# Attention values on four column tiles, built on chip: one change to a gated cross-attention and routed FFN kernel

## The chip, the cores and the metric

The kernel runs on one core of a Trainium2 chip. The metric is device time in microseconds (us) of one execution, the median of the runs shown. The engines of the core are named as in the profile: PE (TensorE matmuls), PEld (TensorE weight loads), DVE (VectorE), ACT (ScalarE), POOL (GpSimd) and SP (SyncE, which here only issues DMAs).

## The reference

```python
# x: 8 batches x 256 tokens x 256; ctx_768: 8 x 77 keys x 192; 16 heads of 16; FFN hidden 1024; 2 experts
q = (x @ wq + bq).reshape(B, Sq, H, D).transpose(0, 2, 1, 3)
k = (y @ wk + bk).reshape(B, -1, H, D).transpose(0, 2, 1, 3)
v = (y @ wv + bv).reshape(B, -1, H, D).transpose(0, 2, 1, 3)
scores = einsum('bhqd,bhkd->bhqk', q, k) / sqrt(D)
attn = softmax(scores, axis=-1)
out = einsum('bhqk,bhkd->bhqd', attn, v)
out = out.transpose(0, 2, 1, 3).reshape(B, Sq, E) @ wo + bo
# whole model:
x = x + tanh(g_xattn[0]) * xattn(layernorm(x), ctx_768)
x = x + tanh(g_ffn[0]) * ffn(layernorm(x))   # shared FFN + one of two experts per token (top-1 of a gate)
```

All products whose inputs are cut into a high and a low fp32r part take three fp32r matmuls (high by high, low by high, high by low). The scores of batch 0, the key, value and context projections, all transposes and the products with the values take plain fp32.

## The kernel before, in words

Batches are the outer loop of the attention. For each batch the kernel normalises 256 tokens (`nm`), transposes them (`in`), projects queries (`qy`) and then works on four quarters `k` = 0 to 3: two token tiles `t` by two groups `g` of 8 heads. One quarter is a row of 616 = 8 x 77 probabilities per token. Its steps are: scores on PE (`sc`), maxima on DVE (`sm`, L1246), subtraction on DVE (`ss`, L1258) followed by one exponential on ACT (`ex`, L937), or, for the ten quarters in `FOLDED`, eight exponentials of 77 columns on ACT straight out of PSUM (L947), sums and reciprocals on DVE (`su`, L1264 and L1268), and the division on POOL (`di`, L690).

The 616 columns are then cut into five chunks of keys by heads: four of 128 and a middle one of 104. PE transposes each chunk for both token tiles (`tn`, L1668; the probabilities are the stationary operand and the identity matrix is the moving one), two chunks to a PSUM bank, and ACT copies the bank to `pT` (`te`, L956). `attend` (`va`, L1672) multiplies `pT` with a block-diagonal matrix of values `v_diag`: chunks 0 and 1 hold the first four heads of a group, so they need only output columns 0 to 63, and chunks 3 and 4 only columns 64 to 127. The middle chunk holds parts of both and needs all 128 columns. That gives eight matmuls on 64-column tiles of the array and two on all 128 columns, each with 256 moving columns of fp32. ACT and DVE cut the result into high and low parts (`vae`, `val`), and PE projects it (`ou`).

The diagonal layout of the values is made through memory: POOL clears one buffer of `v_diag`, SP writes it to `v_dram` twice (`vz`, L454), writes each batch's values into the diagonal with two DMAs (`vw`, L484), and reads the block back with three (`vr`, L498). The transposed context `yT` lies in the second buffer of `v_diag` until the projections are done. The keys go through `k_dram` too: two DMAs out (`kw`) and eight per batch back in (`kr`, L481).

The order of the work is written out by hand, one list for each engine (L80 to L139). Each engine takes the steps of its list strictly in order. SP's list, around the change, is:

```python
fl.0 kw.0 vz.0 vz.1 kw.1 kr.1 kr.2 wd.0 vw.0 wd.1 vw.1 vr.0 kr.3 vw.2 vr.1 vr.2 kr.4 ...
```

`wd.n` (L516) loads a 1 MB FFN weight. `wd.0` and `wd.1` fill the two halves of `stage` with the shared weights. ACT rounds them in `wh.n` (L1003, its ACTIVATE on L1012), which waits for the load's semaphore. ACT's list around it is:

```python
... te.0.2.0 te.0.3.1 ex.1.2 ine.3.0 wh.1 te.0.4.1 nm.5 ex.1.3 q32.3.0 nm.6 qe.3 ine.4.1 ex.2.0 ex.2.1 vae.0.0 ...
```

and PE's is:

```python
... in.3.0 tn.0.4.1 sc.2.0 qy.3.0 in.4.1 sc.2.1 va.0.0 tn.1.0.1 ...
```

Here `in.4.1` writes the bank that `tn.0.4.1` filled, so it waits until ACT has done `te.0.4.1`. After the attention the shared FFN (`h`, `y`) and then nine rounds of routed FFN follow, up to the end.

Of the kernel before, what the change touches and what calls it, by code (L numbers as in the profile page):

```python
# [5 lines left out]
F32 = mybir.dt.float32  # L6
# [3 lines left out]
ALU = mybir.AluOpType  # L10
# [3 lines left out]
P = 128  # L14
# [24 lines left out]
MIDDLE = CHUNKS // 2  # L39
ROWS = [GK - (CHUNKS - 1) * P if c == MIDDLE else P for c in range(CHUNKS)]  # L40
ROW0 = [sum(ROWS[:c]) for c in range(CHUNKS)]
CK = 96
# [18 lines left out]
SEAM_OPS = 7  # L61

# [74 lines left out]
    fl.0 kw.0 vz.0 vz.1 kw.1 kr.1 kr.2 wd.0 vw.0 wd.1 vw.1 vr.0 kr.3 vw.2 vr.1 vr.2 kr.4 vw.3 wd.3 vw.4 vr.3  # L137
    kr.5 vr.4 wd.2 vw.5 vw.6 vr.5 kr.6 vw.7 ps.0 kr.7 vr.6 vr.7 ps.1 wd.4 wd.5 ps.2 ps.3 xs ps.4
# [24 lines left out]
def build(nc, x, ctx_768, g_xattn, g_ffn, wq, bq, wk, bk, wv, bv, wo, bo,  # L163
          gate_w, w1, b1, w2, b2, sw1, sb1, sw2, sb2, out):
    k_dram = nc.dram_tensor("k_dram", (P, 2 * GROUPS, BATCHES * KEYS), F32).ap()
    v_rows = nc.dram_tensor("v_rows", (2, GK, GROUPS, P), F32)
    v_dram = v_rows.ap()
# [9 lines left out]
    with ctx:  # L177
# [3 lines left out]
        def sb(name, shape, dt=F32, scope=ctx):  # L181
# [99 lines left out]
        yT = v_diag[0:CK + 1, 1, :, :, :].rearrange("p c g f -> p (c g f)")[:, 0:CKC * BATCHES * KEYS].rearrange(  # L281
            "p (k n) -> p k n", k=CKC)
# [46 lines left out]
        v_zeroed = [sem(f"v_zeroed{n}") for n in range(2)]  # L329
        v_out = [sem(f"v_out{n}") for n in range(2)]  # L330
# [108 lines left out]
        def _(sp):  # L439
# [44 lines left out]
            def values_out(b):  # L484

                n = b % 2
                sp.wait_ge(v_32, b // 2 + 1)
                if b < 2:
                    sp.wait_ge(v_zeroed[n], 16 * 2)
                else:  # L490
                    sp.wait_ge(v_in[n], 16 * 3 * (b // 2))
                for g in range(GROUPS):
                    diagonal = bass.AP(v_rows, n * GK * GROUPS * P + g * P,
                                       [[GROUPS * P, KEYS], [KEYS * GROUPS * P + HEAD_DIM, HG], [1, HEAD_DIM]])
                    sp.dma_start(diagonal, v32[:, b // 2, n, g * P:(g + 1) * P].rearrange("k (h f) -> k h f", h=HG)
                                 ).then_inc(v_out[n], 16)

            def values_in(b):  # L498

                n = b % 2  # L500
                sp.wait_ge(v_out[n], 16 * GROUPS * (b // 2 + 1))
                if b == 0:
                    sp.wait_ge(v_zeroed[0], 16 * 2)
                    sp.wait_ge(v_zeroed[1], 16 * 2)
                if b == 1:
                    sp.wait_ge(v_ps, BATCHES // 2)
                if b >= 2:
                    sp.wait_ge(o_ps, b - 1)
                for c in (0, MIDDLE + 1):
                    sp.dma_start(v_diag[:, n, c:c + MIDDLE, :, :].rearrange("p c g f -> p c (g f)"),  # L510
                                 v_dram[n, ROW0[c]:ROW0[c] + MIDDLE * P].rearrange("(c p) g f -> p c (g f)", p=P)
                                 ).then_inc(v_in[n], 16)
                sp.dma_start(v_diag[0:ROWS[MIDDLE], n, MIDDLE, :, :].rearrange("p g f -> p (g f)"),
                             v_dram[n, ROW0[MIDDLE]:ROW0[MIDDLE + 1]].rearrange("p g f -> p (g f)")).then_inc(v_in[n], 16)

# [35 lines left out]
            for step, at in walk(SP_ORDER):  # L551
                if step == "vz":
                    zero_values(*at)
# [4 lines left out]
                if step == "vw":  # L558
                    values_out(*at)
# [48 lines left out]
        def _(pool):  # L608
# [12 lines left out]
            nc.gpsimd.memset(v_diag[:, 0, :, :, :], 0.0).then_inc(cleared[1], 1)  # L621
# [226 lines left out]
        def _(act):  # L848
# [1055 lines left out]
```

## Time and profile before

| | |
|---|---|
| median of 3 runs | 337.58 us (336.97 to 338.42) |
| profiled execution, span from first to last instruction | 339.1 us |
| profiled execution's own time beside its span | not given by the page; the span stands for it, 1.5 us above the median |
| PE busy | 318.2 us (94%) |
| DVE, ACT, POOL busy | 227.9, 215.6, 184.0 us |
| mean granted PE clock | 0.980 |
| DMA | 38150 packets, 35.68 MB; 16608 packets under 512 B |

A busy share is the time in which an engine has an instruction under way, so a busy PE may still have idle columns or tiles. The mean clock of 0.980 comes mainly from one stretch at half rate around 31.8 to 42 us.

### The profile page before, as it was taken

What the parts mean: (1) busy time and instruction counts of PE and PEld (TensorE: products, weight loads), DVE (VectorE), ACT (ScalarE), POOL (GpSimd) and SP (SyncE); (2) the same over time, 40 slices, a digit from 0 to 9 for tenths busy, and PEclk for the clock granted to TensorE, in tenths of its full rate; (3) what the DMA queues carried; (4) which work ended last, traced back from release to release, by engine and by line L of the source; (5) the groups of instructions that cost most, each with busy time, mean ns of one, the idle gap of its engine ahead of it and who ended that gap; (6) DMA issues with size and microseconds to landing.
All of it is one profiled execution on the core that took longest, in us unless ns stands there. A gap on an engine that the chain in (4) does not pass through costs nothing.

```text
span 339.1 us, 7286 instructions
## 1 busy us (share of the span) xinstructions
PE 318.2 (94%) x2363; PEld 282.2 (83%) x2363; DVE 227.9 (67%) x516; ACT 215.6 (64%) x483; POOL 184.0 (54%) x261
## 2 busy tenths in 40 slices
PE   6997879899999999999999999999999999999993
PEld 5764666678988877788799889999999999999992
DVE  6999689999878899796767675534333544353463
ACT  2855898976786665658957584547546546464652
POOL 8226979885652564757371177432255536534542
PEclk9998599999999999999999999999999999999997
DMA  7992855274422030053160100315246233212300
GB/s 191 299 340 38 241 126 160 42 198 128 109 80 56 2 97 29 0 139 121 15 240 2 62 2 31 127 32 188 79 168 217 66 151 93 77 35 75 92 32 28
DMA packets 38150, 35.68 MB, mean 105 GB/s; under 512 B 16608, under 2 KB 35060, under 8 KB 37613
## 3 DMA queue, kind: packets, MB, share of 16 engines
q1 hardware_dynamic: 34568, 27.36, 28.5%
q0 software_dynamic: 2720, 7.32, 6.4%
q10 hardware_dynamic: 837, 0.67, 0.8%
q8 instruction: 14, 0.23, 0.3%
q14 instruction: 11, 0.09, 0.1%
HBM read 21.20 MB, written 9.85 MB: 92 GB/s over the span
## 4 chain that ended last, share of the span: by engine, by line
PE 61%; DVE 15%; ACT 8%; issue 7%; DMA 5%; POOL 1%; POOLq 1%; SPq 1%; DVEq 0%; ACTq 0%
PE y_ps L1535 20%; PE h_ps L1535 17%; PE bank L1535 9%; PE s_ps L1535 9%; DMA x_all<-in_x 5%; PE bank L1668 4%; ACT probs L947 2%; DVE rsum L1264 2%; DVE smax L1246 1%; DVE probs L1258 1%; DVE stats L1147 1%; DVE other_sum L1232 1%; ACT pT L956 1%; DVE hT_lo L1469 1%; ACT xn L898 1%
## 5 line engine op out<-in xcount | busy, mean ns | idle before, releaser
L690 POOL TENSOR_TENSOR probs<-probs,rinv 128x616 f32<-128x616 f32 x32 | 39.1, 1223 | 37.8 <-DVE rinv L1268 37.5
L1535 PE MATMUL y_ps<-sw,hT_hi 128*128 128x256 f32 x272 | 57.1, 290 | 1.2 <-DVE hT_lo L1513 1.2
L1535 PE MATMUL y_ps<-ew,hT_hi 128*128 128x256 f32 x256 | 54.1, 286 | 1.8 <-DVE hT_lo L1469 1.7
L1469 DVE TENSOR_TENSOR hT_lo<-h,hT_hi 128x256 fp32r<-128x256 f32 x64 | 29.2, 457 | 38.5 <-ACT h L1086 35.2
L1535 PEld LDWEIGHTS y_ps<-sw,hT_hi 128*128 128x128 f32 x272 | 44.9, 191 | 2.9 <-DVE hT_lo L1513 1.8
L1535 PEld LDWEIGHTS y_ps<-ew,hT_hi 128*128 128x128 f32 x256 | 42.4, 188 | 3.0 <-DVE hT_lo L1469 3.0
L1535 PE MATMUL h_ps<-x2T_hi,sw 128*128 128x512 f32 (+1 forms) x160 | 43.6, 359 | 0.1
L1083 ACT ACTIVATE hT_hi<-h_ps,vec_cols 128x256 fp32r<-128x256 f32 x32 | 15.2, 475 | 39.5 <-PE h_ps L1535 35.3
L995 ACT ACTIVATE hT_hi<-h_ps,vec_cols 128x512 fp32r<-128x512 f32 (+1 forms) x40 | 24.6, 614 | 21.9 <-PE h_ps L1535 17.3
L1535 PE MATMUL y_ps<-sw,hT_lo 128*128 128x256 f32 x136 | 38.4, 282 | 0.0
L1535 PE MATMUL y_ps<-ew,hT_lo 128*128 128x256 f32 x128 | 35.9, 280 | 0.0
L1264 DVE TENSOR_REDUCE rsum<-probs 128x8 f32<-128x616 f32 x32 | 25.1, 785 | 9.3 <-ACT probs L947 5.9
L821 POOL DMA_INDIRECT out<-final,scatter_token x16 | 18.0, 1127 | 24.6 <-DVE final L1488 19.2
L1535 PEld LDWEIGHTS h_ps<-x2T_hi,sw 128*128 128x128 f32 x160 | 26.8, 190 | 3.5 <-issue 0.8
L716 POOL TENSOR_TENSOR hT_lo<-h,hT_hi 128x512 fp32r<-128x512 f32 (+1 forms) x15 | 17.2, 1151 | 21.9 <-ACT h L1000 21.7
L1535 PE MATMUL h_ps<-x2T_lo,sw 128*128 128x512 f32 (+1 forms) x80 | 27.8, 348 | 0.0
L956 ACT ACTIVATE pT<-bank 128x512 f32<-128x512 f32 x40 | 23.7, 611 | 5.9 <-PE bank L1668 5.4
L1535 PE MATMUL h_ps<-xsT_parts,ew 128*128 x192 | 26.5, 280 | 0.0
L1535 PE MATMUL s_ps<-xsT_parts,ew 128*128 x192 | 26.4, 279 | 0.0
L1379 DVE TENSOR_TENSOR hT_lo<-h,hT_hi 128x512 fp32r<-128x512 f32 (+1 forms) x25 | 16.2, 654 | 15.0 <-ACT h L1000 15.0
L1535 PEld LDWEIGHTS y_ps<-sw,hT_lo 128*128 128x128 f32 x136 | 26.0, 191 | 0.2
L1668 PE MATMUL bank<-ident,probs 128*128 128x128 f32 (+1 forms) x160 | 24.3, 284 | 1.4 <-ACT pT L956 1.0
(206 smaller groups left out, 837.1 us busy)
## 6 DMA issues: line engine op xcount, KB each, us to landing
v_diag<-v_rows SPq DMA_DIRECT2D x16, 256.0 KB
stage<-in_L_ffn_w SPq DMA_DIRECT2D x4, 1024.0 KB, 5.6
sw<-ew SPq DMA_DIRECT2D x4, 1024.0 KB
xs<-sorted_dram SPq DMA_DIRECT2D x8, 257.0 KB
stage<-in_L_ffn_sw SPq DMA_DIRECT2D x2, 1024.0 KB, 6.6
x_all<-in_x SPq DMA_DIRECT2D x1, 1536.0 KB, 9.8
part_dram<-x_all SPq DMA_DIRECT2D x3, 512.0 KB, 2.9
k_dram<-probs SPq DMA_DIRECT2D x2, 616.0 KB, 5.9
```

The lines of the kernel that those rows point to most:

```text
L690: nc.gpsimd.tensor_tensor(pq, pq, rinv[:, b % 2, k, :].unsqueeze(2).to_broadcast([P, HG, KEYS]), ALU.mult).then_inc(p_ready, 1)
L716: nc.gpsimd.tensor_tensor(hT[1][:, q % HB, 0:width], h32[:, q % 2, 0:width], hT[0][:, q % HB, 0:width], ALU.subtract).then_inc(h_lo_pool, 1)
L821: pool.indirect_dma_start(out=out[:, :], out_offset=bass.IndirectOffsetOnAxis(ap=scatter_token[:, t:t + 1], axis=0), in_=final[:, t, :], i ...
L947: ins = nc.scalar.activation(to[:, h * KEYS:(h + 1) * KEYS], score_banks(quarter)[:, h // HH, keys], ACT.Exp, bias=smax[:, b % 2, k, h:h + 1])
L956: nc.scalar.activation(pT[:, 2 * u:2 * u + 2, :].rearrange("p c s -> p (c s)"), bank[m][:, :], ACT.Copy).then_inc(pT_sb, 1)
L995: nc.scalar.activation(hT[0][:, q % HB, 0:width], h_ps[:, q % 2, 0:width], ACT.Relu, bias=b1_sb[:, 0, c:c + 1]).then_inc(h_hi, 1)
L1083: nc.scalar.activation(hT[0][:, c % HB, 0:RTOK], hidden_bank(c % 4)[:, 0:RTOK], ACT.Relu, bias=b1_sb[:, 1 + e, c:c + 1]).then_inc(h_hi, 1)
L1264: nc.vector.tensor_reduce(out=rsum[:, b % 2, k, :], in_=probs[:, b % 2, k, :].rearrange("p (h k) -> p h k", k=KEYS), axis=AX_X, op=ALU.add ...
L1379: nc.vector.tensor_tensor(hT[1][:, q % HB, 0:width], h32[:, q % 2, 0:width], hT[0][:, q % HB, 0:width], ALU.subtract).then_inc(h_lo, 1)
L1469: nc.vector.tensor_tensor(hT[1][:, c % HB, 0:RTOK], h32[:, c % 2, 0:RTOK], hT[0][:, c % HB, 0:RTOK], ALU.subtract).then_inc(h_lo, 1)
L1535: return nc.tensor.matmul(out_, lhsT, rhs, start=start, stop=stop, **kw)
L1668: ins = nc.tensor.transpose(bank[m][0:ROWS[c], v * SEQ + t * P:v * SEQ + (t + 1) * P], probs[:, b % 2, g * TB + t, ROW0[c]:ROW0[c] + ROWS[ ...
```

## The change

Heads are taken in pairs. One group of 8 heads has four pairs, and a pair has 154 = 128 + 26 key columns. The keys of two pairs are interleaved in `probs`: the column of (pair, head in pair, key) is `n * 308 + q * 154 + k * 2 + i`, with `n` the half of the group, `i` the pair in that half and `q` the head in the pair. Subtraction, exponentials, sums and division address `probs` through this layout. The first (or last) 128 keys of each pair are now every second column, and the middle 104 columns are what is left of all four pairs. The transposes read their four chunks of 128 with a step of two elements.

`attend` then has, per group, four matmuls on four 32-column tiles of the array (one per pair, with 128 rows) and one on all 128 columns with 104 rows. That is again eight and two matmuls a batch.

The values are no longer written to memory. POOL clears `v_pair` and `v_left` once, and SP copies each batch's values from `v32` in SBUF to their places with eight DMAs (four for `v_pair`, four for `v_left`), in runs of 16 elements. `vz` and `vw` are gone, `yT` has a buffer of its own, and SP's list has `vr.0 vr.1` between `wd.0` and `wd.1`. The lists of the other engines are unchanged.

```diff
 SP_ORDER = """
-    fl.0 kw.0 vz.0 vz.1 kw.1 kr.1 kr.2 wd.0 vw.0 wd.1 vw.1 vr.0 kr.3 vw.2 vr.1 vr.2 kr.4 vw.3 wd.3 vw.4 vr.3
-    kr.5 vr.4 wd.2 vw.5 vw.6 vr.5 kr.6 vw.7 ps.0 kr.7 vr.6 vr.7 ps.1 wd.4 wd.5 ps.2 ps.3 xs ps.4
+    fl.0 kw.0 kw.1 kr.1 kr.2 wd.0 vr.0 vr.1 wd.1 kr.3 vr.2 kr.4 wd.3 vr.3 kr.5 vr.4 wd.2 vr.5 kr.6 ps.0 kr.7
+    vr.6 vr.7 ps.1 wd.4 wd.5 ps.2 ps.3 xs ps.4
 """
...
+        def heads_of(b, k):
+            return probs[:, b % 2, k, :].rearrange("p (n q k i) -> p n i q k", n=2, q=2, i=HP)
+        def by_head(rows):
+            return rows.rearrange("p (n i q) -> p n i q", n=2, q=2)
...
             def values_in(b):
                 n = b % 2
-                sp.wait_ge(v_out[n], 16 * GROUPS * (b // 2 + 1))
...
-                for c in (0, MIDDLE + 1):
-                    sp.dma_start(v_diag[:, n, c:c + MIDDLE, :, :] ..., v_dram[n, ...]).then_inc(v_in[n], 16)
-                sp.dma_start(v_diag[0:ROWS[MIDDLE], n, MIDDLE, :, :] ..., v_dram[n, ...]).then_inc(v_in[n], 16)
+                sp.wait_ge(cleared[1], 2)
+                sp.wait_ge(v_32, b // 2 + 1)
+                if b >= 2:
+                    sp.wait_ge(o_ps, b - 1)
+                split = P - KEYS
+                for half, parity, to, key in ((0, 0, 0, 0), (0, 1, KEYS, 0), (1, 0, 0, LEFT), (1, 1, split, 0)):
+                    rows = KEYS if half == parity else split
+                    heads = v32[key:key + rows, b // 2, n, half, :].rearrange("k (c q f) -> k c q f", q=2, f=HEAD_DIM)
+                    cols = slice(parity * HEAD_DIM, (parity + 1) * HEAD_DIM)
+                    sp.dma_start(v_pair[to:to + rows, n, half, :, cols], heads[:, :, parity, :]).then_inc(v_in[n], 16)
+                for half in range(2):
+                    key = split if half == 0 else 0
+                    left = v32[key:key + LEFT, b // 2, n, half, :].rearrange("k (g d) -> k g d", g=GROUPS)
+                    for i in range(HP):
+                        first = (2 * i + 1 - half) * HEAD_DIM
+                        rows = slice(half * HP * LEFT + i, (half + 1) * HP * LEFT, HP)
+                        sp.dma_start(v_left[rows, n, :, half * HR + first:half * HR + first + HEAD_DIM],
+                                     left[:, :, first:first + HEAD_DIM]).then_inc(v_in[n], 16)
...
             def turn(b, u, m):
+                        if c < PAIRS:
+                            first = c // HP * (GK // 2 + HP * LEFT) + c % HP
+                            cols = slice(first, first + HP * (P - 1) + 1, HP)
+                        else:
+                            cols = slice(HP * P, HP * P + ROWS[c])
...
             def attend(b, m):
                 for g in range(GROUPS):
-                    for n in range(MIDDLE):
-                        for half in range(2):
-                            c, cols = half * (MIDDLE + 1) + n, slice(half * HR, (half + 1) * HR)
-                            mm(bank[m][cols, g * SEQ:(g + 1) * SEQ], v_diag[:, b % 2, c, g, cols],
-                               pT[:, g * CHUNKS + c, :], g == 0 and n == 0, False, skip_group_check=True)
+                    for i in range(PAIRS):
+                        cols = slice(i * PD, (i + 1) * PD)
+                        mm(bank[m][cols, g * SEQ:(g + 1) * SEQ], v_pair[:, b % 2, i // HP, g * HP + i % HP, :],
+                           pT[:, g * CHUNKS + i, :], g == 0, False, skip_group_check=True)
```

## Rows read from the trace of the kernel before

**Rows 1.** The page: busy time of each engine; granted PE clock in 40 slices.
```profile
PE 318.2 (94%) x2363; PEld 282.2 (83%) x2363; DVE 227.9 (67%) x516; ACT 215.6 (64%) x483; POOL 184.0 (54%) x261
...
PEclk9998599999999999999999999999999999999997
```
**Rows 2.** The chain of waits: shares, then pieces (start us, us, what).
```profile
PE 61%; DVE 15%; ACT 8%; issue 7%; DMA 5%; POOL 1%; POOLq 1%; SPq 1%; DVEq 0%; ACTq 0%
...
74.73 2.94 PE bank L1535 x20
...
80.70 0.44 PE bank L1668 x4
...
84.50 0.72 PE y_ps L1535 x6
...
186.38 2.94 PE bank L1535 x20
```
**Rows 3.** Busy time by stretch; then PEclk, DMA share, GB/s.
```profile
26.60:31.80 5.20, 3.35 (x12) 1.81 (x10) 4.91 (x12) 2.60 (x9) 3.69 (x14) 1.00 0.20 32
31.80:42.00 10.20, 7.96 (x38) 6.82 (x40) 7.60 (x13) 8.30 (x23) 9.37 (x12) 0.50 0.73 193
...
45.60:78.00 32.40, 28.80 (x222) 21.64 (x219) 29.46 (x49) 27.58 (x59) 28.60 (x40) 1.00 0.48 118
78.00:113.00 35.00, 35.00 (x273) 30.69 (x273) 29.92 (x62) 26.65 (x64) 16.53 (x27) 1.00 0.36 89
113.00:151.00 38.00, 36.69 (x269) 30.18 (x269) 33.21 (x83) 21.73 (x44) 23.24 (x32) 1.00 0.23 59
151.00:228.00 77.00, 77.00 (x548) 69.41 (x547) 49.59 (x114) 50.67 (x100) 39.04 (x56) 1.00 0.21 69
```
**Rows 4.** Timeline of PE (start us, us): value projection, last attend, what follows it.
```profile
16.91 1.90 PE L1535 MATMUL y_ps<-stage,v_diag 97*77 97x256 f32 x8
...
186.31 3.01 PE L1535 MATMUL bank<-pT,v_diag 128*64 128x256 f32 x20
188.97 0.82 PE L1535 MATMUL h_ps<-x2T_hi,sw 128*128 128x512 f32 x2
```
**Rows 5.** Groups by form: busy us, mean ns of one, idle before.
```profile
L690 POOL TENSOR_TENSOR probs<-probs,rinv 128x616 f32<-128x616 f32 x32 | 39.1, 1223 | 37.8 <-DVE rinv L1268 37.5
L1264 DVE TENSOR_REDUCE rsum<-probs 128x8 f32<-128x616 f32 x32 | 25.1, 785 | 9.3 <-ACT probs L947 5.9 <-ACT probs L937 3.3
...
L1668 PEld LDWEIGHTS bank<-ident,probs 128*128 128x128 f32 x128 | 15.4, 144 | 3.5 <-issue 1.2 <-ACT pT L956 0.8 <-DVE x2T_lo L1293 0.5
...
L1535 PEld LDWEIGHTS y_ps<-sw,hT_hi 128*128 128x128 f32 x256 | 41.9, 191 | 0.9 <-issue 0.5
```
**Rows 6.** Timeline of SP's DMA issues (start us, us), 22 to 41 us.
```profile
22.61 11.74 SPq L481 DMA_DIRECT2D k_own<-k_dram  x16
34.45 0.53 SPq L530 DMA_DIRECT2D stage<-in_L_ffn_sw  x1
35.08 0.89 SPq L495 DMA_DIRECT2D v_rows<-v  x2
36.02 2.38 SPq L530 DMA_DIRECT2D stage<-in_L_ffn_sw  x1
38.50 2.24 SPq L495 DMA_DIRECT2D v_rows<-v  x2
```
**Rows 7.** Weight loads into `stage`: issue to landing.
```profile
DMA to landing us min/median/max: 4.9/5.7/8.0
```
**Rows 8.** Timeline of ACT around `wh.1` (start us, us).
```profile
45.12 0.60 ACT L907 ACTIVATE xnT_hi<-bank 128x512 fp32r<-128x512 f32 x1
45.60 1.92 ACT L1012 ACTIVATE sw<-stage 128x2048 fp32r<-128x2048 f32 x1
47.40 0.61 ACT L956 ACTIVATE pT<-bank 128x512 f32<-128x512 f32 x1
```
**Rows 9.** Timeline of PE: `in.4.1`, which needs the copy after `wh.1`.
```profile
48.10 0.62 PE L1607 MATMUL bank<-ident,xn 128*128 128x128 f32 x4
```

More of the change, by code:

```diff
@@ L37 @@
 TURNS = GROUPS * CHUNKS // 2
-MIDDLE = CHUNKS // 2
-ROWS = [GK - (CHUNKS - 1) * P if c == MIDDLE else P for c in range(CHUNKS)]
-ROW0 = [sum(ROWS[:c]) for c in range(CHUNKS)]
+PAIRS = HG // 2
+HP = PAIRS // 2
+PK = 2 * KEYS
+LEFT = PK - P
+ROWS = [P] * PAIRS + [PAIRS * LEFT]
+PD = 2 * HEAD_DIM
 CK = 96
@@ L61 @@
 SEAM_OPS = 7
+VALUE_LOADS = 4 + PAIRS
 UNITS = [[0], [1, 2], [3, 4], [5, 6], [7]]
@@ L328, in build @@
         v_32 = sem("v_32")
-        v_zeroed = [sem(f"v_zeroed{n}") for n in range(2)]
-        v_out = [sem(f"v_out{n}") for n in range(2)]
         v_in = [sem(f"v_in{n}") for n in range(2)]
@@ L482, in keys_in @@
                                  ).then_inc(k_in[n], 16)
[L484 to L496, printed above, removed]
@@ L557, in _ @@
                     keys_in(*at)
-                if step == "vw":
-                    values_out(*at)
                 if step == "vr":
@@ L688, in divide @@
                 pool.wait_ge(p_rinv, 4 * b + k + 1)
-                pq = probs[:, b % 2, k, :].rearrange("p (h k) -> p h k", k=KEYS)
-                nc.gpsimd.tensor_tensor(pq, pq, rinv[:, b % 2, k, :].unsqueeze(2).to_broadcast([P, HG, KEYS]),
-                                        ALU.mult).then_inc(p_ready, 1)
+                pq = heads_of(b, k)
+                inverse = by_head(rinv[:, b % 2, k, :]).unsqueeze(4).to_broadcast([P, 2, HP, 2, KEYS])
+                nc.gpsimd.tensor_tensor(pq, pq, inverse, ALU.mult).then_inc(p_ready, 1)
             def scatter(u):
@@ L887, in value_rows @@
                 act.wait_ge(v_ps, j + 1)
-                nc.scalar.activation(v32[:, j, :, :].rearrange("k n d -> k (n d)"), value_bank(j), ACT.Copy
+                nc.scalar.activation(v32[:, j, :, :, :].rearrange("k n m d -> k (n m d)"), value_bank(j), ACT.Copy
                                      ).then_inc(v_32, 1)
@@ L946, in exponents @@
                     keys = slice(h % HH * KEYS, (h % HH + 1) * KEYS)
-                    ins = nc.scalar.activation(to[:, h * KEYS:(h + 1) * KEYS], score_banks(quarter)[:, h // HH, keys],
+                    ins = nc.scalar.activation(heads_of(b, k)[:, h // HH, h % HH // 2, h % 2, :],
+                                               score_banks(quarter)[:, h // HH, keys],
                                                ACT.Exp, bias=smax[:, b % 2, k, h:h + 1])
@@ L1008, in weights_hi @@
                     for half in range(2):
-                        act.wait_ge(v_out[half], 16 * GROUPS * BATCHES // 2)
+                        act.wait_ge(v_in[half], 16 * VALUE_LOADS * BATCHES // 2)
                 if n >= 4:
@@ L1256, in shifted @@
                 dve.wait_ge(s_max, 4 * b + k + 1)
-                m = smax[:, b % 2, k, :].rearrange("p (n h) -> p n h", n=2).unsqueeze(3).to_broadcast([P, 2, HH, KEYS])
-                nc.vector.tensor_tensor(probs[:, b % 2, k, :].rearrange("p (n h k) -> p n h k", n=2, k=KEYS),
-                                        score_heads(4 * b + k), m, ALU.subtract).then_inc(s_shifted, 1)
+                m = by_head(smax[:, b % 2, k, :]).unsqueeze(4).to_broadcast([P, 2, HP, 2, KEYS])
+                nc.vector.tensor_tensor(heads_of(b, k), score_heads(4 * b + k).rearrange("p n (i q) k -> p n i q k", q=2),
+                                        m, ALU.subtract).then_inc(s_shifted, 1)
             def sums(b, k):
                 dve.wait_ge(p_exp, 4 * b + k + 1)
-                nc.vector.tensor_reduce(out=rsum[:, b % 2, k, :],
-                                        in_=probs[:, b % 2, k, :].rearrange("p (h k) -> p h k", k=KEYS),
-                                        axis=AX_X, op=ALU.add).then_inc(p_sum, 1)
+                nc.vector.tensor_reduce(out=by_head(rsum[:, b % 2, k, :]), in_=heads_of(b, k), axis=AX_X, op=ALU.add
+                                        ).then_inc(p_sum, 1)
                 dve.wait_ge(p_sum, 4 * b + k + 1)
@@ L1596, in values_in @@
                         ins = mm(value_bank(j)[:, n * DIM:(n + 1) * DIM], yT[rows, k, b * KEYS:(b + 1) * KEYS],
-                                 wv_sb[rows, k, :], k == 0, k == CKC - 1)
+                                 wv_sb[rows, k, :].rearrange("p (g m d) -> p m g d", g=GROUPS, m=2), k == 0,
+                                 k == CKC - 1)
                 ins.then_inc(v_ps, 1)
```

40 lines of the change are left out of this document (10 added, 30 removed).

## The prediction, made before the changed kernel was run

> **What bounds the kernel now.** I read the page first, then the chain of waits, then the busy time by stretch, and last the timelines of PE, SP and ACT around the edited steps. PE is busy for 94% of the span and the others for 54 to 67% [rows 1], and 61% of the chain is PE [rows 2]. By stretch it differs [rows 3]. From 45.6 to 78 us nobody leads: PE is busy 28.8 of 32.4 us, DVE 29.5, ACT 27.6, POOL 28.6, so a delay of any of them is handed on. From 78 to 113 and from 151 to 228 us PE is never idle. From 113 to 151 PE has 1.3 us idle in 38, DVE is busy 33.2, and the chain there runs mostly over DVE. After 228 us comes the routed FFN, which the change doesn't touch.
>
> **PE's part of the change.** Each attend has 20 matmul records (two to an fp32 matmul). The last one begins at 186.31 and the next step at 188.97, so it takes 2.66 us [rows 4]. One fp32 record of 256 columns alone in the array costs 0.217 us: eight records of the value projection take 1.90, the last being 0.38 long, and (1.90 - 0.38) / 7 = 0.217 [rows 4]. Twenty in a row would take 4.34 us. At 2.66 the sixteen 64-column records must run in pairs: 8 slots + 4 full ones = 12 slots x 0.217 = 2.60. On four 32-column tiles the sixteen records fit 4 slots, plus 4 full ones: 8 x 0.217 + 0.06 = 1.80. Each attend saves 0.86 us at full clock. The trace shows no four tiles at once, so the bounds are 0 (only two run together) and 0.86; I take 0.86, because two tiles overlap without loss.
>
> The eight attends save 6.9 us of PE time, but not all of it reaches the end. Four of them lie whole on the chain (74.7, 95, 165 and 186 us, of which the first and last stand in [rows 2]): 4 x 0.86 = 3.4 us. The other four lie in the stretches where other engines share the bound [rows 3]; there PE would mostly wait longer. I count a quarter of their 3.4: 0.9. Sum -4.3 us, with bounds 0 and -6.9.
>
> The Trainium skill, TensorE: Matmul & The Clock Gate, "Part 3: Packing small matmuls", gives 2.38 times for three column tiles, not 3. At that efficiency (estimated 79% for four) the sixteen records would take 1.08 instead of 0.86 us and an attend would save 0.65; the sum of the four on the chain would be -2.6 instead of -3.4. The trace's pairs lose nothing, so I stay with the rows.
>
> **The step of two elements.** The stationary loads of 128 of the 160 transposes now read every second element. Now such a load takes 144 ns [rows 5] and transposes follow each other every 0.11 us (0.44 for 4), while a load of 191 ns [rows 5] goes with a spacing of 0.12 us (0.72 for 6) [rows 2]. If the step made the load as slow as that, each transpose would cost 0.01 more: 1.3 us in all, at most. Below nothing there is no reason. The other readers and writers of `probs` are 32 sums of 785 ns, 32 divisions of 1223 ns [rows 5], the subtractions and exponentials. No row has a stepped access, so their bounds are nothing and a doubling of the sums, 25 us of DVE. I take nothing, since number of elements and engine stay the same. The Trainium skill, SBUF — State Buffer, "SBUF: two separate sides", says that two hits per 16-byte line keep full rate; a step of 8 bytes gives exactly two. By that rule the cost is nothing too, but one element further it would not be.
>
> **SP's part, where the change can lose.** Removed: four clearing writes, sixteen diagonal writes, 24 reads of `v_dram`. Added: 64 small copies, eight per batch. Their bytes are nothing (DMA share is 0.2 to 0.5 after 78 us [rows 3]), but SP's issue time and order count. Now SP issues the 16 key DMAs from 22.61 to 34.35, `wd.0` at 34.45, two `vw` at 35.08 and `wd.1` at 36.02 [rows 6]. Afterwards:
>
> - The key DMAs start when `kw.0` has landed instead of behind `vz`, about 1.2 us earlier (21.4), and at their undisturbed pace of 0.635 instead of 11.74 / 16 = 0.73 end at 31.6. So `wd.0` goes out at 31.6, 2.9 us earlier.
> - Then 16 value copies stand before `wd.1`, instead of two. Their price is between 0.45 each (0.89 for two `vw`) and 1.12 (2.24 for two `vw` behind the weights) [rows 6]. Both ends of a copy have three dimensions, as a key DMA has, so I take 0.635: 10.2 us, and `wd.1` goes out at about 42.4 (39.3 to 50).
> - A weight load lands 4.9 to 8.0 us after its issue [rows 7]. With nearly nothing beside it I take 5.4: landing at 47.8.
>
> `wh.1` on ACT needs that load. It runs at 45.60, directly behind other work, so it waits for nothing now [rows 8]. At 47.8 ACT stands for 2.2 us. Behind it on ACT are `te.0.4.1` (47.40), then `nm.5`, `ex.1.3` and the queries; PE's `in.4.1` (48.10 [rows 9]) needs that copy's bank, and the attend of batch 0 comes after it. From there the engines run in lockstep [rows 3]; I let 85% through: +1.9 us. Bounds: 0 (issue at 0.45) and about +8 (every copy at twice its pace).
>
> `kr.3` behind `wd.1` goes out at about 43 against 44 to 45 now. The later copies (`vr.2` on) wait for an attend two batches before their use and have some 10 us or more; 5 us of issue each fit. POOL's clearing has 1024 elements instead of 1280. Nothing else moves. `vr.0` and `vr.1` land before 50 us, where the first attend needs them.
>
> **Sum.** -4.3 + 1.9 = -2.4 us. The profiled span is 339.1, 1.5 above the median of 337.58; the same difference on the median gives **335.2 us**.
>
> **Rivals.**
> - *The weight load comes on time.* The copies cost SP about 0.45 each and `wd.1` lands before 45.6. For it: `vw` went at that pace. Against: their neighbours with two strided sides don't. Only the gain is left: 337.6 - 4.3 = 333.3, to 330.7 if all eight attends count.
> - *The stall grows and takes the clock along (slower).* Copies blocked behind `wd.0`, as `wd.1` and the second `vw` are now (2.38 and 2.24 us [rows 6]), put `wd.1` at 44.5 and its landing at 50: ACT stands 4.4 us, +3.7. PE is then idle from 48.3 for over 4 us. Now, PE was idle 1.85 of 5.2 us before 31.8, and the granted clock was 0.50 (the 1.2 GHz level) for the next 10.2 us [rows 3]. The same again costs half of some 8.5 us of PE work less what was slack, about +3. Result 337.6 - 4.3 + 3.7 + 3 = 340.0. It decides from a `wd.1` issue later than about 43.5 us. Against: the 3.6 us of idle spread over 45.6 to 78 us left the clock at 1.00 [rows 3].
> - *Four tiles run no better than two.* No gain, stall stays: 339.5. For it: no row has four. Against: pairs lose nothing.
> - *The stepped access costs.* A tenth more on sums and divisions and 0.01 on each transpose: 32 x 0.08 + 32 x 0.12, half of it hidden by idle time before them, + 1.3 gives +4: 339.2. Against: none but the absence of any row for it.
>
> **How the numbers follow.** Chances: forecast 0.36, load on time 0.24, stall with clock 0.20, tiles don't overlap 0.08, stepped access 0.12. The range goes from 331.5 (nearly all attends count, no stall) to 341 (stall, clock, and some of the last two). About 0.5% (1.7 us) is what a measurement of this kernel tells from no change, so faster means under 335.9 and slower over 339.3. Faster: 0.27 of the forecast's 0.36, and the 0.24 of the load on time, 0.51. Slower: 0.15 of the clock case, 0.06 and 0.08 of the last two, 0.29. Same: the rest, 0.20.
>
> **What would show it.** In the profile after: each attend 1.80 us from its first record to the next step; transpose loads still near 144 ns and spaced 0.11; `rsum` near 785 and the division near 1223 ns; SP's issue of `wd.1` at about 42.4 and 0.635 per copy; ACT idle about 2.2 us before L1012 at 46 us, with a DMA as releaser; PE's clock 1.00 after 42 us; PE never idle from 78 to 113 us, moved as a whole. The prediction is wrong if the clock falls a second time, if the attends keep 2.66 us, or if 113 to 151 us takes the gain back over DVE.

## The result, and the profile after

The changed kernel took 348.64 us (median of 4 runs, 348.31 to 349.12), the kernel before 338.0 beside it (336.97 to 340.12). The ratio is 1.0318, with a 95% interval of 1.0272 to 1.0363: slower by some 10.6 us, where 335.2 with a range of 331.5 to 341.0 was forecast. The profiled execution of the changed kernel took 349.12 us, 1.8 more than its span of 347.3. (In nearly all other runs on record, too, the time lies 1.7 to 1.9 us above the span. So the execution in the profile of before took about 340.9, and is one of that kernel's slower ones.)

The page after, its first two parts, cut to the rows that answer to [rows 1]:

```profile
PE 317.8 (91%) x2363; PEld 282.0 (81%) x2363; DVE 230.0 (66%) x516; ACT 215.8 (62%) x483; POOL 183.0 (53%) x262
...
PE   7998572989899999899999999999999999999993
...
PEclk9999896999999999999999999999999999999998
DMA  6951422014130102003225010130553362213201
```

PE is busy for as long as before (317.8 against 318.2 us) in a span that is 8.2 us longer, so the loss is idle time. It lies mostly in the seventh slice (52 to 61 us), where PE's digit is 2 and the clock's 6. The chain of waits there has what the chain of before did not have, SP's copies and a weight load (start, duration in us, engine, target):

```profile
48.02 0.83 SPq L501
48.90 7.19 DMA stage<-in_L_ffn_sw
56.31 1.62 issue
```

SP's DMA issues of the changed kernel (start us, us), which answer to [rows 6], and ACT around `wh.1` (now L998), which answers to [rows 8]:

```profile
33.40 0.52 SPq L518 DMA_DIRECT2D stage<-in_L_ffn_sw  x1
34.02 4.36 SPq L494 DMA_DIRECT2D v_pair<-v  x4
38.43 3.47 SPq L501 DMA_DIRECT2D v_left<-v  x4
42.01 3.33 SPq L494 DMA_DIRECT2D v_pair<-v  x4
45.37 3.48 SPq L501 DMA_DIRECT2D v_left<-v  x4
48.90 0.52 SPq L518 DMA_DIRECT2D stage<-in_L_ffn_sw  x1
```

```profile
47.86 0.60 ACT L892 ACTIVATE xnT_hi<-bank 128x512 fp32r<-128x512 f32 x1
56.12 1.91 ACT L998 ACTIVATE sw<-stage 128x2048 fp32r<-128x2048 f32 x1 [7.65 <-DMA stage<-in_L_ffn_sw]
57.93 0.58 ACT L942 ACTIVATE pT<-bank 128x512 f32<-128x512 f32 x1
```

Sixteen value copies took SP from 34.02 to 48.90, 0.93 us each. `wd.1` was issued at 48.90 instead of 36.02, and ACT stood for 7.65 us for it, with everything behind it in ACT's order. PE's timeline shows the same hole, and the busy time by stretch shows what the clock did (columns: stretch, length, busy PE, PEld, DVE, ACT, POOL, PEclk, DMA share, GB/s):

```profile
58.57 1.11 PE L1593 MATMUL bank<-ident,xn 128*128 128x128 f32 x4 [7.56 <-ACT pT L942]
```

```profile
41.60:45.00 3.40, 3.40 (x18) 3.18 (x20) 2.00 (x4) 2.98 (x9) 3.40 (x5) 0.50 0.12 12
...
48.40:55.20 6.80, 2.04 (x18) 1.61 (x14) 3.10 (x6) 0.06 (x1) 3.93 (x5) 1.00 0.59 173
55.20:62.10 6.90, 3.41 (x22) 2.07 (x26) 1.83 (x4) 5.98 (x10) 0.86 (x1) 0.51 0.04 8
```

PE was busy 2.04 of 6.8 us, and then the granted clock fell to the 1.2 GHz level until 62.1. The first such stretch, 10.2 us long in [rows 3], was 3.4 us here, and a second profile of the kernel before (e5 below) has none at all. Where and how long the clock falls early in the kernel differs from one execution to the next.

The attends' own matmuls are as short as forecast, at full clock and with four tiles at once. The groups by form, which answer to [rows 5] (busy us, mean ns of one, idle before):

```profile
L676 POOL TENSOR_TENSOR probs<-probs,rinv 128x616 f32<-128x616 f32 x32 | 39.5, 1237 | 46.7 <-DVE rinv L1253 46.3
L1250 DVE TENSOR_REDUCE rsum<-probs 128x8 f32<-128x616 f32 x32 | 25.2, 786 | 17.2 <-ACT probs L922 11.2 <-ACT probs L932 5.9
...
L1659 PEld LDWEIGHTS bank<-ident,probs 128*128 128x128 f32 x128 | 18.2, 206 | 6.1 <-ACT pT L942 3.1 <-DVE x2T_lo L1278 1.1 <-issue 0.9
...
L1520 PE MATMUL bank<-pT,v_pair 128*32 128x256 f32 x128 | 9.1, 406 | 0.1
```

```profile
73.25 1.07 PE L1520 MATMUL bank<-pT,v_pair 128*32 128x256 f32 x16
74.25 1.13 PE L1520 MATMUL bank<-pT,v_left 104*128 104x256 f32 x4
```

The four full-width records begin 1.00 us after the first of the sixteen, and a chain piece of an attend fell from 2.94 [rows 2] to 2.06 us. Sum and division kept their durations. The stepped loads went from 144 to 206 ns.

Where the difference arises, by landmarks of the profiles (us from the span's start, all read from timelines):

| | before | before, again | after | after, again | e1, `wd.1` first |
|---|---|---|---|---|---|
| first scores of batch 1 | 32.39 | 31.89 | 35.74 | 33.38 | 33.04 |
| `wh.1` on ACT | 45.60 | 43.74 | 56.12 | 54.96 | 45.59 |
| attend of batch 0 | 50.37 | 48.49 | 60.87 | 59.72 | 50.36 |
| fourth store of a part | 228.35 | 226.13 | 238.83 | 237.71 | 228.27 |
| from the attend to that store | 177.98 | 177.64 | 177.96 | 177.99 | 177.91 |
| end | 339.1 | 334.7 | 347.3 | 345.2 | 336.9 |

Everything is lost before the attend of batch 0: 10.5 us in the first pair of profiles, 11.2 in the second. What `wh.1` is late (10.52 us in the first pair) arrives whole at the attend (10.50) and at the last store (10.48). From there to the last store, where 6.9 us of attends were to be saved, the two kernels need the same time within 0.4 us. The routed stage behind it has nothing of the change. It took 107.2 to 110.8 us in the profiles of both kernels, and explains nothing.

### The profile page after: what moved, and what is told of

It is laid out like the page before. It is cut to its first block, busy times and chain, and to the rows that moved or that the text cites. A ratio compares the mean times of both kernels' runs of the same rounds, so it can differ in the third digit from the quotient of the medians.

```text
span 347.3 us, 7297 instructions
## 1 busy us (share of the span) xinstructions
PE 317.8 (91%) x2363; PEld 282.0 (81%) x2363; DVE 230.0 (66%) x516; ACT 215.8 (62%) x483; POOL 183.0 (53%) x262
## 4 chain that ended last, share of the span: by engine, by line
PE 54%; DVE 15%; ACT 8%; issue 8%; SPq 7%; DMA 5%; POOL 1%; POOLq 1%; DVEq 0%; ACTq 0%
PE y_ps L1520 21%; PE h_ps L1520 16%; PE s_ps L1520 7%; PE bank L1520 5%; SPq L479 3%; PE bank L1659 3%; DVE rsum L1250 2%; SPq L494 2%; DMA stage<-in_L_ffn_sw 2%; SPq L501 2%; ACT probs L932 2%; DVE smax L1232 2%; DMA stage<-in_ctx 2%; DVE other_sum L1218 1%; DVE probs L1244 1%
## 5 line engine op out<-in xcount | busy, mean ns | idle before, releaser
L676 POOL TENSOR_TENSOR probs<-probs,rinv 128x616 f32<-128x616 f32 x32 | 39.5, 1237 | 46.7 <-DVE rinv L1253 46.3
L1520 PE MATMUL y_ps<-ew,hT_hi 128*128 128x256 f32 x256 | 53.1, 285 | 0.8 <-DVE hT_lo L1454 0.8
L1454 DVE TENSOR_TENSOR hT_lo<-h,hT_hi 128x256 fp32r<-128x256 f32 x64 | 29.5, 461 | 32.3 <-ACT h L1072 32.0
L1250 DVE TENSOR_REDUCE rsum<-probs 128x8 f32<-128x616 f32 x32 | 25.2, 786 | 17.2 <-ACT probs L922 11.2
L1659 PE MATMUL bank<-ident,probs 128*128 128x128 f32 (+1 forms) x160 | 25.6, 291 | 2.4 <-ACT pT L942 1.6
L1659 PEld LDWEIGHTS bank<-ident,probs 128*128 128x128 f32 (+1 forms) x160 | 21.0, 191 | 6.8 <-ACT pT L942 3.1
```

Source lines behind the costliest of these rows:

```text
L676: nc.gpsimd.tensor_tensor(pq, pq, inverse, ALU.mult).then_inc(p_ready, 1)
L1250: nc.vector.tensor_reduce(out=by_head(rsum[:, b % 2, k, :]), in_=heads_of(b, k), axis=AX_X, op=ALU.add).then_inc(p_sum, 1)
L1454: nc.vector.tensor_tensor(hT[1][:, c % HB, 0:RTOK], h32[:, c % 2, 0:RTOK], hT[0][:, c % HB, 0:RTOK], ALU.subtract).then_inc(h_lo, 1)
L1520: return nc.tensor.matmul(out_, lhsT, rhs, start=start, stop=stop, **kw)
L1659: ins = nc.tensor.transpose(bank[m][0:ROWS[c], v * SEQ + t * P:v * SEQ + (t + 1) * P], probs[:, b % 2, g * TB + t, cols], ident[:, :])
```

## The experiments

Fourteen runs were made. The kernel before ran beside each of them, with medians from 336.75 to 339.45 us by group of runs (e1 to e4, e5 to e8, e9 to e12, e13 and e14), so across groups only ratios are compared. Line numbers are those of the kernel in question.

**e1 and e11: `wd.1` back in its place.**

```diff
-    fl.0 kw.0 kw.1 kr.1 kr.2 wd.0 vr.0 vr.1 wd.1 kr.3
+    fl.0 kw.0 kw.1 kr.1 kr.2 wd.0 wd.1 vr.0 vr.1 kr.3
```

> The changed kernel with one word moved in SP's order: wd.1 goes out directly behind wd.0, ahead of the 16 value copies of vr.0 and vr.1. My theory: the loss is the late weight load (ACT idle 7.65 us before sw<-stage) and the second stretch at half clock that the idle PE brings (55.3 to 62.1 us, worth 3.4). Without it wd.1 is issued near 36, ACT does not wait for it, PE's clock stays at full speed after its first dip, and the time falls from 348.6 by 9 to 11 us to 338 to 340. If the slower start (everything 3 us later at 16 us) is an accident of single executions, 335.5 to 338. Rival: the stall only moves, because the copies now hold back kr.3 and the first attend waits for its values; then no more than half of it goes, 343 or more.

338.69 us, ratio 1.0041 (1.0012 to 1.0071) instead of 1.0318. One word in SP's list gives back 2.8% of the time, some 9.4 us. ACT's timeline of this kernel has no wait before `wh.1`:

```profile
45.59 1.92 ACT L998 ACTIVATE sw<-stage 128x2048 fp32r<-128x2048 f32 x1
```

The copies, now behind the weight load, hold nothing up, so the rival falls. On another chip, with a second profile:

> The kernel with wd.1 first once more, beside the two others on one chip, as their measure and for a second profile of its start. By all theories the ratio of before, 1.004 with 0.003 to either side, and SP past the second load of x at 9.2 to 11.

Ratio 1.0048 (1.0025 to 1.0071), as expected. The 0.4 to 0.5% that stay are real, and with the shorter attends they had to be explained: the sum of the forecast would have this kernel at 333.3.

**e2: half of the copies ahead.** `wd.0 vr.0 wd.1 vr.1`.

> The changed kernel with 8 value copies (vr.0) ahead of wd.1 and 8 (vr.1) behind it. At the 0.93 to 0.98 us per copy that the first eight took, wd.1 is issued at about 41.9 and lands at 47.5 to 49; ACT comes to it at about 48.4. My theory (a threshold: only a load later than ACT's turn costs) says that this is within 1 us of the kernel with wd.1 first. Rival (every copy ahead of the weights costs, since they share SP and the DMA rings): halfway between the two, 343 to 344.

340.14 us, ratio 1.0093 (1.0057 to 1.0128), 1.45 over e1, so it was not quite free and a little outside the 1 us of the theory; the rival's 343 is far off. `wd.1` went out at 41.40 and `wh.1` ran at 46.99, 1.34 us late:

```profile
46.99 1.91 ACT L998 ACTIVATE sw<-stage 128x2048 fp32r<-128x2048 f32 x1 [1.34 <-DMA stage<-in_L_ffn_sw]
```

That the loss is about the stall is chance, though. In this execution the clock fell from 51.4 to 58 us, over the attend of batch 0 and what follows it:

```profile
51.40:58.00 6.60, 6.25 (x32) 3.88 (x33) 5.57 (x11) 5.51 (x10) 5.89 (x7) 0.50 0.17 27
```

From that attend to the next it took 13.57 us instead of the 12.34 of e1, and the fourth store of a part stood at 230.92, 2.65 later than in e1: 1.39 from the stall and 1.23 from the clock. The routed stage, which has nothing of the edit, happened to be 1.35 shorter (107.3 against 108.6). The threshold picture holds, and the point is an issue at about 40 us, since from issue to ACT's copy it took 5.6 us here and ACT's turn comes at 45.6.

**e3: the same delay in the kernel before.** Nothing but `wd.1` is later.

```diff
-    wd.0 vw.0 wd.1 vw.1 vr.0 kr.3
+    wd.0 vw.0 vw.1 vr.0 kr.3 wd.1
```

> The kernel before, with wd.1 moved behind vw.1, vr.0 and kr.3: nothing else is later, only this weight load, issued at about 48 instead of 36 as in the changed kernel. My theory: ACT idles 7 to 9 us before sw<-stage, PE's clock falls to half a second time, and the time rises by 9 to 11 us to 347 to 349. Rival (the changed kernel's loss comes from its copies, stepped accesses or start, and the weight load has slack behind it): at most 3 us, 341 or less.

347.08 us, ratio 1.0297 (1.024 to 1.0354): the late weight load alone makes 9.8 us, where the whole change makes 10.6. Its ACT and PE show the stall and the attend of batch 0 at half clock:

```profile
53.73 1.91 ACT L1012 ACTIVATE sw<-stage 128x2048 fp32r<-128x2048 f32 x1 [8.85 <-DMA stage<-in_L_ffn_sw]
```

```profile
58.48 4.77 PE L1535 MATMUL bank<-pT,v_diag 128*64 128x256 f32 x20
```

The records of this attend span 4.77 us against 3.01 at full clock, and the stretch from it to the next attend was 13.87 us, not 12.35. In the changed kernel the clock falls too, but that stretch is 12.38 us, as with e1 (12.34), and from `wh.1` to the attend it is 4.75 us in it and 4.77 in e1. So the fall of the clock behind the stall cost 1.5 us in e3 and nothing in the changed kernel. What differs in these four profiles, beside the longer attend of e3, is how far the fall reaches beyond the start of the attend: 1.2 us in the profile of after and 1.7 in its repeat, where it cost nothing, and 3.7 in e3 and 6.3 in e2, where it cost 1.5 and 1.2.

**e7: every attend as long as before.** The 16 records on column tiles are issued twice, the second time over the first.

```diff
-                for g in range(GROUPS):
+                for g in [*range(GROUPS)] * 2:
                     for i in range(PAIRS):
```

> The kernel with wd.1 first, with the 16 records on four column tiles of every attend issued twice, the second time over the first: an attend then takes about 2.66 us as in the kernel before, +0.86 each, 6.9 us of PE in all. Theory: nearly all of the attends' gain was hidden, because DVE (its 3.35 us sw<-stage,sw, and the softmax work from 113 to 151 us) ends just behind PE; the time rises by only 0 to 2 us over 338.7, so up to 340.7. Rival (my prediction's step: four attends whole on the chain and a quarter of the rest): +4.3, 343. If all eight are on the path: +6.9, 345.6.

338.5 us, ratio 1.0009 (0.9973 to 1.0045), where e1 and e11 had 1.0041 and 1.0048. So 6.9 us more of PE's work cost nothing that can be measured, the low end of the theory's 0 to 2. The forecast's 4.3 us would have needed a ratio near 1.017 and are excluded. The third attend shows how. In e1, then in e7, PE (and DVE in e1) around it:

```profile
74.72 1.07 PE L1520 MATMUL bank<-pT,v_pair 128*32 128x256 f32 x16
75.72 1.13 PE L1520 MATMUL bank<-pT,v_left 104*128 104x256 f32 x4
77.77 0.47 PE L1520 MATMUL h_ps<-x2T_hi,sw 128*128 128x256 f32 x2 [0.92 <-DVE sw L1382]
...
73.72 3.35 DVE L1382 TENSOR_TENSOR sw<-stage,sw 128x2048 fp32r<-128x2048 f32 x1
76.99 0.68 DVE L1278 TENSOR_TENSOR x2T_lo<-bank,x2T_hi 128x512 fp32r<-128x512 f32 x1
```

```profile
75.10 1.93 PE L1520 MATMUL bank<-pT,v_pair 128*32 128x256 f32 x32
...
76.97 1.13 PE L1520 MATMUL bank<-pT,v_left 104*128 104x256 f32 x4
78.19 0.48 PE L1520 MATMUL h_ps<-x2T_hi,sw 128*128 128x256 f32 x2
```

From the attend's first record to the next step it is 3.05 us with short attends, 3.09 with doubled ones and 3.12 in the kernel before. In the kernel before PE seemed to set the pace without a gap, but DVE's `x2T_lo`, behind the subtraction, ended at 77.68, 0.1 us before PE's next step at 77.78. In e1 it ended at 77.67, again 0.1 us before that step. The last attend is alike. In e1 the next step comes 2.22 us after its first record, not 1.80, 0.1 us behind the end of an `x2T_lo` at 188.96. With doubled attends it comes after 2.65.

**e4: what the step of two costs.**

```diff
-                            cols = slice(first, first + HP * (P - 1) + 1, HP)
+                            cols = slice(c * P, (c + 1) * P)
```

> The kernel with wd.1 first whose 128 transposes of whole chunks read contiguous columns instead of every second one; the pairs of heads are then mixed up, so what is left out is the right order of the keys. Prices the step of two: the loads fall from 206 to about 144 ns. My theory: this costs the chain at most 0.01 to 0.02 us a transpose, 1.3 to 2.5 us in all, so 0 to 2 us faster than the kernel with wd.1 first. Rival (the slower load sets PE's pace wherever transposes stand alone): 62 ns on each of 128, 5 to 8 us faster.

337.1 us, ratio 1.0007 (0.9967 to 1.0048), 1.6 us under e1. The load's row:

```profile
L1659 PEld LDWEIGHTS bank<-ident,probs 128*128 128x128 f32 x128 | 14.3, 140 | 7.4 <-ACT pT L942 3.4 <-DVE xnT_lo L1225 1.3 <-DVE x2T_lo L1278 1.1
```

So the step makes a load 66 ns slower (206 against 140). PE's eight transposes in a row took 0.96 us to the next step in e1 and 0.85 here, 0.014 each, or 1.8 us over all 128 if none is hidden. In the trace, though, 1.17 of the gain lie in one stretch, between the third and the fourth attend (20.24 against 19.07 us), and most of it is no transpose: the sixteen stepped ones of a stretch make 0.22 at 0.014 each. In e1 POOL ran a division beside DVE's subtraction (73.72, 3.35 us, above). That division, then the same two in e4:

```profile
73.68 1.23 POOL L676 TENSOR_TENSOR probs<-probs,rinv 128x616 f32<-128x616 f32 x1
```

```profile
73.42 2.30 DVE L1382 TENSOR_TENSOR sw<-stage,sw 128x2048 fp32r<-128x2048 f32 x1
...
73.51 3.29 POOL L676 TENSOR_TENSOR probs<-probs,rinv 128x616 f32<-128x616 f32 x1
```

One of the two ran at its usual duration, and the other took 1.0 or 2.1 us longer. In e1 POOL was 0.04 us ahead, in e4 DVE 0.09. The pair meets like this in 15 of the 16 profiles (all but e8). DVE took 3.34 to 3.40 us wherever POOL began earlier or at most 0.01 later, and POOL took 3.29 to 3.33 wherever DVE was 0.03 or more ahead. The unchanged kernel before shows both orders: 20.23 us for the stretch in its first profile, where DVE waited, and 19.85 in its second, where POOL did. So the order alone is worth 0.4. And e4, with POOL waiting and short attends, has 19.07 where the kernel before with POOL waiting has 19.85: there the shorter attend shows almost whole (0.78 of 0.86), while with DVE waiting it shows nothing (20.24 against 20.23). That is read from traces; no run fixes the order.

**e8: DVE's subtraction of the weights ahead.**

```diff
-    sm.3.2 ss.3.2 wl.0 n2l.0.0.0
+    wl.0 sm.3.2 ss.3.2 n2l.0.0.0
```

> The kernel with wd.1 first, and DVE's wl.0 (sw<-stage,sw, 3.35 us at 73.7) put ahead of sm.3.2 and ss.3.2, 1.6 us of softmax work. PE waits 0.92 us for it behind the third attend. Theory: PE's wait there goes, and the gain of that attend shows: 0.5 to 0.9 us less, 337.8 to 338.2, more if DVE also starts ahead of POOL's division (with contiguous transposes it started 0.09 us ahead of it and took 2.30 instead of 3.35 us). Rival: the later softmax holds back the next attend, and the time stays at 338.7 or rises by up to 1.6.

340.35 us, ratio 1.0062 (1.0023 to 1.01), so no gain over e1 (1.0041) and perhaps a loss. The subtraction took 2.39 us now, but the stretch from the second to the third attend went from 12.02 to 14.24 us, because PE waits for the softmax that was put behind it:

```profile
76.81 0.41 PE L1520 MATMUL s_ps<-k_own,q_hi 64*128 64x308 f32 x2 [2.05 <-DVE probs L1244]
```

The granted clock then fell to 0.50 (77.4 to 80.7 us), and the first sixteen records of the third attend took 1.87 us instead of 1.00. The rival was right. On DVE, with 29.5 of 32.4 us busy [rows 3], the 3.35 us can't be moved for nothing.

**e5 and e6: both kernels once more, for the start.**

> The kernel before, unchanged, profiled once more, to see what one execution differs from the next. In the profiled execution of before the routed stage (from the last store of a part, 228.35, to the end) took 110.75 us, against 107.2 to 108.6 in four others. If that is chance of single executions it takes 107 to 109 here, and the first attend may begin 1 to 3 us earlier or later than 50.4, with the phase of the clock. If it belongs to the kernel before, 110 to 111 again.

Its time was 336.5 us; the routed stage took 108.6, so the 110.75 was chance.

> The changed kernel, unchanged, profiled once more, for its start: in its profiled execution PE ran its first 14 us at half rate (h_ps<-yT,stage 2.26 us for 4, against 1.20 to 1.28 in the four others) and everything stood 3 us later at 16 us. If that is chance, h_ps takes about 1.2 here and the first keys are stored near 16 us. If it belongs to the change, 2.26 and 18.8 again. The ACT idle before sw<-stage: near 7.7 in either case, or up to 10 when the start is early, since SP's queue is bound by its own issues after 34 us.

Its time was 346.99 us. PE's slow start (matmuls at twice their duration, while the profile gives a granted clock of 1.00) was chance as well. The first keys went out at 16.45. The ACT wait was 9.63 us, near the upper figure: the earlier ACT comes to `wh.1`, the longer it waits, because SP has its own pace.

A smaller delay of the start stayed. In all seven profiles of changed kernels so far (after, its repeat, e1, e2, e4, e7, e8) SP passed its wait on the second load of `x` at 9.15 to 10.99 us. In three of the kernel before or its variant (before, e5, e3) it was 8.14 to 9.26. POOL clears 1024 columns where it cleared 1280, so its loads of bias and gate rows start at 5.60 instead of 5.77. Four more kernels vary when these loads start.

**e9, e10, e12, e14: POOL's loads later; e13: earlier.** The edit of e9 and e14, in the kernel of e1 (e10 has it four times; e12 has two clearings of `v_diag` more in the kernel before):

```diff
+            for n in range(1):
+                nc.gpsimd.memset(v_left[:, :, :, :], 0.0).then_inc(held, 1)
+                pool.wait_ge(held, n + 1)
```

> The kernel with wd.1 first, with one more clearing of v_left (0.46 us of POOL) ahead of POOL's loads. What is open: with wd.1 first the time is still 1.4 us over before. In three profiles of before SP passed its wait on the second load of x at 8.1 to 9.3 us, in seven of the changed kernel at 9.2 to 11.0, and the first scores come 1 us later. POOL clears 1024 columns instead of 1280 and so starts its row loads at 5.60 instead of 5.77. Theory: those 768 KB get ahead of parts of the x load; with the extra clearing they start 0.3 us later than in before, SP passes at 8.1 to 9.3 and the time falls by about 1.3 us to that of before (ratio 1.000). Rival: the order of 0.17 us has nothing to do with it; SP passes at 9.2 to 11 and the ratio stays 1.004.

> The same with four more clearings (about 2.2 us of POOL). Theory: as with one, and perhaps a little more, since the x load then has the DMA engines to itself: ratio 0.996 to 1.000. Against it: the row loads and the gains then land late, and ACT waits for the gains. Rival: ratio 1.004 or more.

> The kernel before with its clearing of v_diag done three times (2.2 us more of POOL) ahead of POOL's loads, to see whether their start matters to that kernel too. Theory: its x load is already ahead, so nothing to 0.5 us is gained (ratio 0.998 to 1.001). Rival: the row loads are needed late only and any delay of them helps, ratio 0.996 or less; or the later gains cost, 1.002 or more.

> The kernel before, in which POOL clears only 1024 of the 1280 columns of v_diag ahead of its row loads, as the changed kernel clears 1024, and the rest behind them. Theory (the row loads get ahead of the second load of x): POOL's row loads start near 5.55 instead of 5.77, SP passes its wait on that load at 9.2 to 11 instead of 8.1 to 9.3, the first scores come at 32.7 to 33.7 instead of 31.9 to 32.8, and the time rises by about 1 us (ratio 1.002 to 1.004). Rival (what delays the start is something else in the changed kernel, where its tiles lie for one): start and ratio as before, 1.000.

> The kernel with wd.1 first and one more clearing ahead of POOL's loads, again, beside e13. Theory: SP passes at 8.1 to 9.3 and the first scores at 31.9 to 32.5, as in its first profile (8.73 and 32.18); the ratio 1.000 to 1.003, against 1.0041 and 1.0048 without the clearing. Rival: 1.004 or more, and the early start of the first profile was chance.

| | row loads start | SP past the second x load | first scores | ratio |
|---|---|---|---|---|
| e13, before, clears 1024 first | 5.55 | 9.99 | 33.42 | 1.0031 (1.0004 to 1.0058) |
| e1 | 5.60 | 9.65 | 33.04 | 1.0041 (1.0012 to 1.0071) |
| e11 | 5.60 | 9.70 | 32.86 | 1.0048 (1.0025 to 1.0071) |
| before, again | 5.78 | 8.27 | 31.89 | 1 |
| e9 | 6.19 | 8.73 | 32.18 | 1.0028 (1.0001 to 1.0056) |
| e14 | 6.18 | 9.13 | 32.45 | 1.0019 (0.9995 to 1.0044) |
| e10 | 7.97 | 8.25 | 32.69 | 1.0043 (1.0012 to 1.0074) |
| e12, before | 8.25 | 9.04 | 32.80 | 1.0001 (0.9973 to 1.003) |

The rows behind the first and the fifth line, SP, POOL and ACT of e13, then of e9:

```profile
9.99 0.39 SPq L452 DMA_DIRECT2D x_all<-in_x  x1
...
5.55 0.57 POOL L643 DMA_DIRECT2D gate_rows<-in_L_ffn_gate_w  x1
...
9.32 0.63 ACT L872 ACTIVATE wqo_hi<-stage 128x512 fp32r<-128x512 f32 x1 [1.54 <-DMA stage<-in_L_xattn_wq]
```

```profile
8.73 0.38 SPq L460 DMA_DIRECT2D x_all<-in_x  x1
...
6.19 0.57 POOL L632 DMA_DIRECT2D gate_rows<-in_L_ffn_gate_w  x1
...
7.95 0.62 ACT L859 ACTIVATE wqo_hi<-stage 128x512 fp32r<-128x512 f32 x1
```

In nine profiles with the row loads before 5.65 us the wait ended at 9.15 to 10.99, in seven with them at 5.77 or later at 8.14 to 9.26. SP's wait is only a mark of the traffic. What an engine waits for in eight of the nine is the query weight `wq`, a load of 256 KB that SP issues at 2.5 us: ACT's `wqo_hi` waits 0.34 to 1.76 us for it, and not in any of the seven. (In the ninth, e4, the second x load itself is the latest of all, 10.99.) Put into the kernel before, the earlier loads made it slower (e13, 1.0031, an interval just clear of 1; its theory held). Both runs of the kernel with half a microsecond of delay (e9 and e14) lie under e1 and e11, but the intervals overlap; e14 is as its theory had it, and the 1.000 expected of e9 did not come. A delay of 2 us gives nothing more (e10, where the theory's 0.996 to 1.000 failed and its rival of 1.004 was right; e12, as expected): the first scores then come at 32.7 to 32.8 although the x load is early. So the direction rests on the profiles and on e13. The size, 1 us in the profiles, is within the intervals of the times.

No version beat the kernel before. Of the changed ones with the right order of the keys e7, with its doubled attends, has the lowest ratio (1.0009), then e14 (1.0019), and the times tell neither from it. A layout that shortens the attends without the step of two was not run.

## Why the prediction was wrong

- **What bounds the kernel: wrong.** "From 78 to 113 and from 151 to 228 us PE is never idle" was read as PE being the bound. e7 refutes it for the whole: with 0.86 us more of PE's work in each of the eight attends the time is the same. A shorter attend turned into waits: behind DVE's `sw` (0.92 us, third attend) and for DVE's `x2T_lo` (0.65 us after the sixth, against 0.23 in the kernel before). In e1 only the last two attends gave something, about half of their 0.86 each.
- **The attend's own cost: right.** 1.80 forecast, 0.86 saved; measured 2.06 against 2.94 in the chain, 0.88. The rival of two tiles falls. By the estimate from the 2.38 times of the Trainium skill, TensorE: Matmul & The Clock Gate, "Part 3: Packing small matmuls", the sixteen records would have taken 1.08 us (0.868 / 0.79 is 1.10); they took 1.00 to the next record, between that and the 0.87 of full overlap. The second sixteen of e7 add 0.87 (1.87 for 32), so all but 0.13 us overlaps fully.
- **Its effect: the step that failed first.** "Four of them lie whole on the chain", −4.3 us in all. Measured: nothing that can be told from zero. By stretches from one attend to the next, e1 against e7: −0.42 and −0.54 behind the last two attends, +0.55 between the fifth and the sixth, about nothing elsewhere. The +0.55 comes on DVE. In before and e7 three `other_sum` operations took 1.52 us and the four behind them 2.48. In e1 the three took 2.54 and the four 2.03, with POOL's `q_lo` at 125.19 in between. That is read from traces; no run moved POOL there.
- **SP's copies: the mis-sized term, and most of the miss.** `wh.1` was forecast 2.2 us late (47.8 instead of 45.6) and started at 56.12, 10.5 late. Of the 8.3 us between, 4.7 are the copies: 0.635 us each was taken from the key DMAs, with bounds of 0.45 and 1.12, and it was 0.93 (`v_left` 0.87, `v_pair` 0.83 to 1.09). Another 1.8 is the start of the copies (34.02 instead of 32.2) and 1.8 the landing (7.19 us instead of 5.4 for this load; in the repeat it took 5.6). The issue at 48.9 instead of 42.4 lay inside the bounds of 39.3 to 50, but past the point where ACT waits each further microsecond counts in full.
- **"I let 85% through": wrong, all of it went through.** 10.52 us at `wh.1`, 10.50 at the attend, 10.48 at the last store; in e2, 1.40 and 1.39 at the first two.
- **The rival "The stall grows and takes the clock along"** named the mechanism, and its point of decision (an issue later than 43.5) was passed by 5 us. It priced it at 340.0, since it stopped at an issue at 44.5 and took a gain of 4.3 off. Its clock term of +3 was nothing in the changed kernel. With the measured 10.5 us of delay, without the gain and without the clock it gives 348.1, and 348.64 was measured.
- **The stepped access: sums and divisions right, the transposing loads wrong.** I let them grow from 144 to 191 at most; they took 206. Per transpose it was 0.014 against the 0.01 allowed. (The rival's sum was off by itself: 3.2 + 1.3 is 4.5, not 4.) The rule cited from the Trainium skill, SBUF — State Buffer, "SBUF: two separate sides" (two hits per 16-byte line keep full rate), held for the engines (rsum 786 against 785 ns), and this load did not keep its duration.
- **POOL's clearing: the step costed at nothing.** "POOL's clearing has 1024 elements instead of 1280. Nothing else moves." What stood behind it on POOL, 768 KB of loads, moved up by 0.17 us and into the way of the `wq` load and the second x load, for about 1 us. With that and key DMAs of 0.67 us each instead of 0.635, `wd.0` came at 33.40, not at 31.6, and still at 33.23 in e1, where PE did not start slowly.

## What to carry to other kernels

Before an engine that is always busy is called the bound, ask of each stretch what its neighbours would show if it were 1 us faster: a neighbour in lockstep with it takes the gain (DVE was busy 87 to 91% of 45.6 to 78 and 113 to 151 us here). Doubling the work in question is a cheap test of that, and can be run before a change is made. Small DMAs on an in-order queue are paid by the issue (0.83 to 1.09 us each for these copies): put them behind every load that an engine waits for, and count what each edit does to the loads at the start.

## What was not expected of the hardware

- Four fp32 matmuls of 256 columns on four 32-column tiles overlap nearly fully: sixteen records in 1.00 us and 32 in 1.87 (e7), against 3.47 for sixteen one after the other (16 x 0.217, from [rows 4]).
- A transposing load with a step of two fp32 elements took 206 ns instead of 140 to 144, while DVE's stepped sums took 786 ns against 785 and POOL's stepped divisions 1237 against 1223.
- Two operations, one of DVE and one of POOL, that begin within 0.1 us of each other on SBUF operands don't share. One waits: 3.35 us instead of 2.30 for DVE, or 3.29 instead of 1.23 for POOL, and 0.03 us in the start decides which.
- A granted clock of 0.51 over 6.9 us cost nothing, where PE was fed by others (4.75 us from `wh.1` to the attend, 4.77 at full clock). In e2 half rate reached 6.3 us beyond the attend's start, and it cost 1.2 us.
